# One transformer layer: the last attention group finished behind its last values, and the sequence branch worked by halves of the tokens

## The chip, the cores and the metric

One core of a Trainium2 chip runs the whole layer in one launch. The metric is device time in microseconds, lower is better. Engines: TensorE (matmul, transpose; PE in the profile), VectorE (DVE), ScalarE (ACT), GpSimd (POOL), SyncE (SP, which issues most DMAs). Each engine works through its own queue in order and waits on semaphores; nothing reorders the program but the person who wrote it.

## The reference

All data are float32: x is 2 x 1024 x 256 (two sequences of 1024 tokens).

```
c  = mixture(x, cond)                 # top 2 of 4 experts per sequence, plus a shared expert
q, k, v = split(c @ w_qkv.T)          # 16 heads of 16; q, k root-mean-square normed
y  = softmax(q k.T / 4) v
y  = y - (y . vn) vn                  # vn = v / |v|
x2 = x + y @ w_proj.T
conv = conv_b + x2[t-1] * cond[0] + x2[t] * cond[1]      # two taps, per channel
b  = softplus(conv @ Wp[:, :64] + bp);  c = tanh(conv @ Wp[:, 64:] + bp)
u  = x2 @ Ws + bs
s[t] = decay * s[t-1] + dt * b[t] * u[t]                 # decay, dt from A_log, dt_log
x3 = (c * s) @ Wo + bo
r  = sigmoid(x3 @ Wr + br);  e = argmax r                # one of 8 experts per token
out = x2 + max(r) * (gelu(x3 @ W1[e]) @ W2[e])
```

## The kernel before

The layer runs in four stages: the mixture with the projection to q, k, v (0 to about 330 us), attention (to 572), the part in question (572 to 651), and the routed experts (to the end).

*Attention.* Eight groups of work, each of four heads of one sequence. A group's output is accumulated in banks 6 and 7 of PSUM, copied to SBUF by VectorE (`take_output`), turned back by TensorE (`turn`), and finished by VectorE (`finish_group`, lines 1311 to 1327: divide by the row sums, product with v, sum, scale, subtract) into `ctx_tm`.

*Output projection and residual.* The 16 tiles of 128 tokens go in eight pairs w = 0 to 7, four to a sequence. For each pair TensorE turns the context (`turn_ctx`, L1788, to bank 0 or 1), ScalarE copies it (L906), TensorE multiplies by the projection (`project`, L1799, to bank 4 or 5), and VectorE adds x in place (`add_x`, L1349). Pairs 0 to 3 belong to the first sequence, whose context was complete long before; pairs 4 to 7 wait for the last group.

*Sequence branch.* `turn_x2(w)` (L1809) turns x2 to channels by tokens, one bank for each pair of channel half `w % 2` and 512 tokens `w // 2`. ScalarE reads each bank twice: the present tap with its bias (L913) and a plain copy (L915). VectorE adds the past tap (`past_tap`, L1037). Then TensorE makes three projections of 2 x 512 tokens: u from x2, b and c from the taps (L1864). The two sequences take the lower and upper 64 partitions, so one instruction of the gates and of the scan works on both sequences, and `n` = 0, 1 is the first and second 512 tokens of both. So both halves of the tokens need pairs of both sequences. The gates use Exp and Ln (softplus) and Tanh on ScalarE; the scan is one VectorE instruction for each half (L1394).

*Logits.* Not x3 but the scan's result times the product Wo x Wr gives the logits (L1897). That product, and the constant part from bo and br, are made by TensorE (L1833 to L1843, bank 0) with ScalarE's copies (L927, L932) and a VectorE add (L1373). Then VectorE routes (from L1402), and x3 is stored and gathered again by expert.

*Order around the change, in the version before.* VectorE's queue: copies of the last group's values, `add_x` 0 to 2, `finish_group`, `add_x` 3, past taps of sequence 0 (1,023 tokens each), `add_x` 4 to 7, past taps of sequence 1, then the gates. TensorE's queue after the last values: pairs 0 to 3 of context and projection, with the last group's turns between; x2 turns 0 to 3; pairs 4 to 7 with x2 turns 4 and 5 between; Wo; x2 turns 6 and 7; the router product; then

```
pe.wait_ge(x2T_out, TT // 2)
for k, w, src in ((1, ws_sb[:], x2T), (0, wp_sb[:, :, 0:N], convT), (2, wp_sb[:, :, N:2 * N], convT)):
    if k == 0:
        pe.wait_ge(conv_done, NB)
        pe.wait_ge(wowr_out, NB + 1)
```

and `keep_warm(9)` (L1850): nine products of constants into bank 6 which nobody reads, each of two matmul instructions in the trace; they keep TensorE busy while VectorE and ScalarE work. The biases of x3 (`bias_x3`, L1874) and the logits stand behind it.

*Transfers.* SP stores x2 when each sequence's residual is done (L601), then loads the weights of four experts (L584, L586), waits for the stores of x3 (issued by ScalarE, L960), and loads the others. GpSimd gathers x3 rows (L724) when the token numbers are known (L1456) and x3 is stored. ScalarE begins to read the experts' weights (L978) behind the stores of x3 in its queue.

Of the kernel before, what the change touches and what calls it, by code (L numbers as in the profile page):

```python
# [40 lines left out]
HG = 4  # L41
# [28 lines left out]
def layer_kernel(nc, a, out):  # L70

    with ExitStack() as ctx:
# [288 lines left out]
        seq_step = sem("seq_step")  # L361
        decay_step = sem("decay_step")
# [390 lines left out]
        def _(act):  # L753
# [163 lines left out]
            for w in range(4):  # L917
                ctx_to_sbuf(w)
            for w in range(4):
                x2_to_sbuf(w)  # L920
            for w in range(4, 7):
                ctx_to_sbuf(w)
            x2_to_sbuf(4)
            x2_to_sbuf(5)
            ctx_to_sbuf(7)
            act.wait_ge(wo_turned, 1)
            act.copy(woT[:].rearrange("p k n -> p (k n)"), bank(0)[:, 0:C]).then_inc(wo_out, 1)  # L927
            x2_to_sbuf(6)
            x2_to_sbuf(7)
            act.wait_ge(wowr_made, 1)  # L930
            for b in range(NB):
                act.copy(wowr[half[b], b, :], bank(0)[half[b], C:C + RE]).then_inc(wowr_out, 1)  # L932


            for n in range(2):
                c = slice(512 * n, 512 * n + 512)
                act.wait_ge(neg_abs, n + 1)
                act.activation(gate_e[:, c], gate_e[:, c], ACT.Exp).then_inc(soft_exp, 1)
            act.wait_ge(decay_e, 1)
            act.activation(decay[:, 2:4], decay[:, 2:4], ACT.Ln, bias=1.0).then_inc(decay_e, 1)  # L940
            for n in range(2):
                c = slice(512 * n, 512 * n + 512)
                act.wait_ge(soft_exp, n + 1)
                act.activation(gate_e[:, c], gate_e[:, c], ACT.Ln, bias=1.0).then_inc(soft_log, 1)
            for n in range(2):
                c = slice(512 * n, 512 * n + 512)
                act.wait_ge(seq_made, 5 + n)
                act.activation(gate_c[:, c], bank(4 + n), ACT.Tanh, bias=bp_c[:, 0:1]).then_inc(tanh_done, 1)
# [76 lines left out]
        def _(dve):  # L1025
# [271 lines left out]

            def take_output(g):
# [47 lines left out]
            def add_x(w):  # L1346
                dve.wait_ge(proj_made, w + 1)
                two = x_tm[:, 2 * w:2 * w + 2, :]
                dve.tensor_tensor(two, bank(4 + w % 2).rearrange("p (i c) -> p i c", i=2), two, ALU.add)\  # L1349
                    .then_inc(x2_done, 1)  # L1350


            def past_tap(b):
                dve.wait_ge(x2T_out, 4 * b + 4)
                for c in range(CK):
                    s = slice(b * L + 1, (b + 1) * L)
                    ins = stt(convT[:, c, s], x2T[:, c, b * L:(b + 1) * L - 1], cond_col[:, c, 0:1],
                              convT[:, c, s], ALU.mult, ALU.add)
                ins.then_inc(conv_done, 1)
# [5 lines left out]
            add_x(3)  # L1365
            past_tap(0)
            for w in range(4, TT // 2):
                add_x(w)
            past_tap(1)


            dve.wait_ge(wowr_out, NB)
            dve.tensor_tensor(blr_row[:], bank(0)[:, C + RE:C + 2 * RE], br_row[:], ALU.add).then_inc(wowr_out, 1)  # L1373
            link = chain(seq_step)
            for n in range(2):
                c = slice(512 * n, 512 * n + 512)
                dve.wait_ge(seq_made, n + 1)
                link(dve.tensor_scalar(seq_u[:, c], bank(2 + n), bs_col[:, 0:1], None, ALU.add))
            for n in range(2):
                c = slice(512 * n, 512 * n + 512)  # L1380
                dve.wait_ge(seq_made, n + 3)
# [3 lines left out]
            dve.wait_ge(decay_e, 2)  # L1385
            link(stt(decay[:, 4:6], decay[:, 0:2], 0.0, decay[:, 2:4], ALU.max, ALU.add))
            link(dve.tensor_tensor(decay[:, 6:7], decay[:, 4:5], decay[:, 5:6], ALU.mult))
            link(dve.tensor_scalar(decay[:, 6:7], decay[:, 6:7], -1.0, 1.0, ALU.mult, ALU.add))
            for n in range(2):
                c = slice(512 * n, 512 * n + 512)  # L1390
                dve.wait_ge(soft_log, n + 1)
                link(stt(gate_b[:, c], gate_b[:, c], 0.0, gate_e[:, c], ALU.max, ALU.add))
                link(stt(gate_b[:, c], gate_b[:, c], decay[:, 5:6], seq_u[:, c], ALU.mult, ALU.mult))
# [3 lines left out]
                dve.tensor_tensor(seq_u[:, c], gate_e[:, c], gate_c[:, c], ALU.mult).then_inc(state_out, 1)  # L1397

# [120 lines left out]
        def _(pe):  # L1519
# [264 lines left out]
            def turn_ctx(w):  # L1784
                pe.wait_ge(ctx_done, 4 if w < 4 else 8)
# [6 lines left out]
            pe.wait_ge(exp_done, UNITS * GROUPS)  # L1792
            turn_ctx(0)
# [19 lines left out]
            for w in range(4):  # L1813
                if w < 3:
                    turn_ctx(w + 1)
                project(w)
                if w == 0:
                    for h in range(2):
                        turn(GROUPS - 1, h)
            for w in range(4):  # L1820
                turn_x2(w)
            turn_ctx(4)
            for w in range(4, TT // 2):
                if w + 1 < TT // 2:
                    turn_ctx(w + 1)
                project(w)
                if w == 5:
                    turn_x2(4)
                    turn_x2(5)
            pe.wait_ge(late_in, 16 * LATE)  # L1830
            pe.wait_ge(ctxT_out, TT // 2)
            for c in range(CK):
                ins = pe.transpose(bank(0)[:, c * P:(c + 1) * P], wo_sb[:, c * P:(c + 1) * P], ident[:])  # L1833
            ins.then_inc(wo_turned, 1)
            turn_x2(6)
            turn_x2(7)
            pe.wait_ge(bo_spread, 1)
            pe.wait_ge(wo_out, 1)
            for c in range(CK):
                ins = pe.matmul(bank(0)[:, C + RE:C + 2 * RE], bo_wide[:, c, :], wr_sb[:, c, :],  # L1840
                                start=(c == 0), stop=(c == CK - 1))
# [175 lines left out]
```

## Time and profile before

| | |
|---|---|
| median of 3 runs | 831.3 us (831.15 to 832.24) |
| profiled execution | 830.84 us |
| its span | 829.1 us |
| PE / DVE / ACT / POOL busy | 95 / 57 / 63 / 30% of the span |
| mean granted clock | 0.99 of full speed |

Times in the rows are microseconds from the span's start. A row of the timeline gives start, duration, engine, line, operation, output<-inputs, shapes and count; in brackets how long the engine had stood idle and what ended it. The duration of several instructions in one row runs from the first one's start to the last one's end. Matmuls overlap, so a busy TensorE is not one at its peak. PEclk is the granted TensorE clock: 1.00 is 2.4 GHz, 0.50 is 1.2 GHz. A float32 matmul of the program is two instructions in the trace.

### The profile page before, as it was taken

The page shows a single profiled execution, that of the slowest core. Times are in us where ns is not written, and L with a number is a line of the kernel's source. Part 1 is how long each engine was busy: PE and PEld are TensorE (multiplying, and loading weights), DVE is VectorE, ACT ScalarE, POOL GpSimd, SP SyncE. Part 2 cuts the span into 40 slices and gives each one's busy share as a digit, 9 for nine tenths or more (in the row PEclk, how much of TensorE's full clock was granted, in tenths as well). Part 3 has the DMA queues.
Part 4 walks back from the last instruction along what each step waited for, and adds up shares of the span by engine and source line. Part 5 has one row for each costly group of instructions (what it writes and reads, how often), then busy time and mean ns, then how long its engine had stood idle before and what let it go on. Part 6 is the DMA issues. An engine that isn't in the chain of part 4 may idle for free.

```text
span 829.1 us, 13128 instructions
## 1 busy us (share of the span) xinstructions
PE 791.7 (95%) x4452; PEld 519.2 (63%) x4452; DVE 468.9 (57%) x865; ACT 523.0 (63%) x696; POOL 248.3 (30%) x308
## 2 busy tenths in 40 slices
PE   8999999998999999999999999999799799999994
PEld 5778888887777877233333233234646488888884
DVE  3887666468866660652321122021466489999994
ACT  4432222463232236999999999996454288888883
POOL 5343444224433410500000001000000356777762
PEclk9999999999999999999999999999999899999999
DMA  9131111100233504055462353100197921111000
GB/s 255 19 71 59 43 35 49 51 23 29 78 126 127 102 17 60 1 77 142 88 128 38 40 77 55 23 1 1 52 326 248 377 79 51 52 49 51 25 11 1
DMA packets 52682, 64.99 MB, mean 78 GB/s; under 512 B 15889, under 2 KB 43929, under 8 KB 52636
## 3 DMA queue, kind: packets, MB, share of 16 engines
q1 hardware_dynamic: 44564, 55.96, 26.9%
q0 software_dynamic: 3312, 6.31, 2.5%
q10 hardware_dynamic: 4760, 2.12, 0.9%
q8 instruction: 27, 0.44, 0.2%
q14 instruction: 19, 0.16, 0.1%
HBM read 51.52 MB, written 15.60 MB: 81 GB/s over the span
## 4 chain that ended last, share of the span: by engine, by line
PE 80%; DVE 9%; ACT 4%; issue 3%; DMA 2%; ACTq 1%; DVEq 1%; POOLq 0%
PE psum L1608 43%; PE psum L1713 15%; PE psum L1700 12%; PE psum L1950 2%; PE psum L1850 2%; DVE w_lo L1481 2%; DVE hl L1037 1%; PE psum L1799 1%; PE psum L1864 1%; DVE hh L1186 1%; PE psum L1671 1%; ACT w_hi L978 1%; DVE ssum L1226 1%; DMA time_bias<-in_L_cond_time_b 1%; DMA xs<-x_d,token_s 1%
## 5 line engine op out<-in xcount | busy, mean ns | idle before, releaser
L824 ACT ACTIVATE pexp<-psum 128x1024 f32<-128x1024 f32 x256 | 238.6, 1151 | 7.6 <-PE psum L1700 7.4
L811 ACT ACTIVATE hid<-psum,b_col 128x512 f32<-128x512 f32 x96 | 66.0, 688 | 160.8 <-PE psum L1608 105.5
L1713 PE MATMUL psum<-pexp,v_ones 128*32 128x512 f32 x1024 | 136.4, 605 | 0.7 <-ACT pexp L824 0.7
L1700 PEld LDWEIGHTS psum<-q_stack,k_stack 48*128 48x128 f32 x512 | 45.6, 183 | 127.0 <-ACT pexp L824 109.3
L1700 PE MATMUL psum<-q_stack,k_stack 48*128 48x512 f32 x512 | 111.5, 480 | 2.9 <-DVE parts L1295 2.9
L1186 DVE TENSOR_SCALAR hh<-hid,scale_col 128x341 fp32r<-128x341 f32 x192 | 71.5, 414 | 69.5 <-ACT hid L811 52.9
L1037 DVE SCALAR_TENSOR_TENSOR hl<-hid,scale_col,hh 128x341 fp32r<-128x341 f32 x192 | 95.4, 538 | 3.4
L1302 DVE COPY yT<-psum 128x512 f32<-128x512 f32 x16 | 11.1, 691 | 131.3 <-PE psum L1713 131.3
L1608 PE MATMUL psum<-hh,w2h 128*128 128x512 f32 x192 | 76.6, 399 | 4.0 <-DVE hl L1037 3.7
L1608 PE MATMUL psum<-x_hi,w1h 128*128 128x512 f32 x192 | 77.0, 401 | 0.6 <-DVE x_lo L1051 0.5
L1608 PE MATMUL psum<-hh,w2l 128*128 128x512 f32 x192 | 75.0, 391 | 0.0
L1608 PE MATMUL psum<-x_hi,w1l 128*128 128x512 f32 x192 | 75.0, 391 | 0.0
L1608 PE MATMUL psum<-hl,w2h 128*128 128x512 f32 x192 | 74.9, 390 | 0.0
L1608 PE MATMUL psum<-x_lo,w1h 128*128 128x512 f32 x192 | 74.9, 390 | 0.0
L666 POOL CAST w1h<-raw 128x256 fp32r<-128x256 f32 x48 | 20.5, 426 | 169.4 <-PE psum L1608 154.3
L1608 PE MATMUL psum<-w_hi,fhT_hi 128*128 128x256 f32 x184 | 55.3, 300 | 5.3 <-DVE fhT_lo L1488 2.7
L1476 DVE TENSOR_TENSOR w_lo<-w_all,w_hi 128x1024 fp32r<-128x1024 f32 x44 | 52.0, 1222 | 10.5 <-ACT w_hi L978 10.5
L1481 DVE TENSOR_TENSOR w_lo<-w_all,w_hi 128x1024 fp32r<-128x1024 f32 x46 | 55.9, 1217 | 0.2 <-ACT w_hi L983 0.2
L690 POOL COPY v_ones<-v_tm 128x512 f32<-128x512 f32 x8 | 4.8, 614 | 167.0 <-PE psum L1713 167.0
L1608 PE MATMUL psum<-w_lo,fhT_hi 128*128 128x256 f32 x184 | 51.5, 280 | 0.0
L1608 PE MATMUL psum<-w_hi,fhT_lo 128*128 128x256 f32 x184 | 51.4, 279 | 0.0
L983 ACT CAST w_hi<-w_all 128x1024 fp32r (+1 forms) x46 | 48.6, 1059 | 0.8 <-PE psum L1608 0.8
(281 smaller groups left out, 1457.9 us busy)
## 6 DMA issues: line engine op xcount, KB each, us to landing
w_all<-in_L_ffn_W SPq DMA_DIRECT2D x16, 1024.0 KB, 13.0
raw<-in_L_cond_ew SPq DMA_DIRECT2D x32, 256.0 KB, 3.1
parts_d<-parts SPq DMA_DIRECT2D x8, 1024.0 KB, 4.1
q_stack<-parts_d SPq DMA_DIRECT2D x48, 128.0 KB, 4.6
k_stack<-parts_d SPq DMA_DIRECT2D x48, 128.0 KB, 7.3
raw<-in_L_cond_sw SPq DMA_DIRECT2D x16, 256.0 KB, 3.6
x_d<-x_tm SPq DMA_DIRECT2D x2, 1024.0 KB, 5.0
x_d<-x_tm ACTq DMA_DIRECT2D x4, 512.0 KB, 3.6
```

What stands on the lines that cost most here:

```text
L666: pool.tensor_copy(w1h[k][:], r1)
L811: act.activation(hid[k % 4][:], bank(k % 4), ACT.Gelu_apprx_tanh, bias=b1_col[:, bass.ds(4 * q + k // 2, 1)]).then_inc(gelu_done, 1)
L824: act.activation(pexp[mt % 2][:, 2 * j:2 * j + 2, 512 * h:512 * h + 512], psum[:, 2 * r:2 * r + 2, :], ACT.Exp, scale=D ** -0.5)\
L983: act.copy(split_quarter(w_hi, 2 + q), quarter(e, 2 + q)).then_inc(w2_hi, 1)
L1037: return dve.scalar_tensor_tensor(out=out, in0=in0, scalar=scalar, in1=in1, op0=op0, op1=op1)
L1186: ins = dve.tensor_scalar(hh[k % 4][:, x0:x1], hid[k % 4][:, x0:x1], w[r], None, ALU.mult)
L1476: dve.tensor_tensor(split_quarter(lo, h), quarter(e, h), split_quarter(hi, h).bitcast(F32), ALU.subtract).then_inc(w1_split, 1)
L1481: dve.tensor_tensor(split_quarter(w_lo, 2 + q), quarter(e, 2 + q), split_quarter(w_hi, 2 + q).bitcast(F32), ALU.subtract).then_inc(w2_spli ...
L1608: ins = pe.matmul(o, w[i], x[j], start=first and n == 0, stop=last and n == 2)
L1700: ins = pe.matmul(psum[:, 2 * r + lane, :], k_stack[i][rows, j, mt * P:(mt + 1) * P], q_stack[i][rows, j, 512 * h:512 * h + 512], start=Tr ...
L1713: ins = pe.matmul(psum[VW * j:VW * j + VW, 6 + h, :], v_ones[i][:, mt, j, :], pexp[mt % 2][:, j, 512 * h:512 * h + 512], start=(mt == 0), ...
L1850: pe.matmul(bank(6), ident[:], projT[:].rearrange("p k c -> p (k c)"), start=(k == 0), stop=(k == n - 1))
```

## The change

`finish_group` takes a function that it calls at two places, so that the last group starts at once and residual adds 0 and 1 stand inside it. Wo and the router product go from behind the pairs to the first pair, in bank 3 in place of bank 0; the x2 turns then wait for the bias row. The pairs go two by two. A past tap is now one channel half of 512 tokens (eight in place of four of 1,023), each counted. The six groups of projections (three kinds, two halves) have each its own waits, and their order is b0, u0, b1, c0, u1, c1. ScalarE takes Exp, Ln and Tanh by halves, and the second half's u (`second_u`), which VectorE made. Nine dummy products become one. The logits of the first half come before the second half is known.

VectorE (behind the bias row the order is residual add 2, 3, past tap 0, 1, add 4, 5, tap 2, 3, add 6, 7, tap 4, 5, and then the gates as shown):

```
-            def finish_group(b, hg):
+            def finish_group(b, hg, between=None):
...
+                if between:
+                    between(0)
                 dve.wait_ge(y_read, 2 * g + 2)
                 dve.tensor_tensor(y_dot[:], y_tm[:], v, ALU.mult).then_inc(post_step, 1)
+                if between:
+                    between(1)
...
+            def past_tap(w):
+                c, s0 = w % 2, 512 * (w // 2)
+                first = 1 if s0 % L == 0 else 0
+                dve.wait_ge(x2T_out, w + 1)
+                stt(convT[:, c, s0 + first:s0 + 512], x2T[:, c, s0 + first - 1:s0 + 511], cond_col[:, c, 0:1],
+                    convT[:, c, s0 + first:s0 + 512], ALU.mult, ALU.add).then_inc(conv_done, 1)

             take_output(GROUPS - 1)
-            for w in range(3):
-                add_x(w)
-            finish_group(1, H // HG - 1)
...
+            finish_group(1, H // HG - 1, between=add_x)
+            dve.wait_ge(wowr_out, NB)
+            dve.tensor_tensor(blr_row[:], bank(3)[:, C + RE:C + 2 * RE], br_row[:], ALU.add).then_inc(wowr_out, 1)
...
+            gate_in(0, first, 1)
+            past_tap(6)
+            past_tap(7)
+            dve.wait_ge(seq_made, 2)
+            link(dve.tensor_scalar(seq_u[:, first], bank(2), bs_col[:, 0:1], None, ALU.add))
+            dve.wait_ge(decay_e, 2)
...
+            gate_in(1, second, 3)
+            states(0, first)
+            states(1, second)
```

ScalarE (behind the evictions, whose order is context 0, 1, Wo, context 2, 3, router product, x2 0, 1, context 4, 5, x2 2, 3, context 6, 7, x2 4 to 7):

```
+            half_exp(0, first)
             act.wait_ge(decay_e, 1)
             act.activation(decay[:, 2:4], decay[:, 2:4], ACT.Ln, bias=1.0).then_inc(decay_e, 1)
...
+            half_log(0, first)
+            half_exp(1, second)
+            output_gate(0, first, 4)
+            half_log(1, second)
+            act.wait_ge(seq_made, 5)
+            act.activation(seq_u[:, second], bank(3), ACT.Identity, bias=bs_col[:, 0:1]).then_inc(second_u, 1)
+            output_gate(1, second, 6)
```

TensorE (between the router product and the wait for the bias row stand context turns 2, 3 and projections 2, 3; behind the wait x2 turns 0, 1, context turns 4, 5, x2 turns 2, 3, projections 4, 5, context turns 6, 7, x2 turns 4, 5, projections 6, 7):

```
+            turn_ctx(0)
+            turn_ctx(1)
+            output_matrix()
+            for h in range(2):
+                turn(GROUPS - 1, h)
+            project(0)
+            project(1)
+            output_times_router()
...
+            pe.wait_ge(wowr_out, NB + 1)
...
+            def sequence(k, n):
+                w, src = ((wp_sb[:, :, 0:N], convT), (ws_sb[:], x2T), (wp_sb[:, :, N:2 * N], convT))[k]
+                pe.wait_ge(x2T_out, 6 if n == 0 else TT // 2)
+                if k != 1:
+                    pe.wait_ge(conv_done, 6 if n == 0 else TT // 2)
...
+            turn_x2(6)
+            turn_x2(7)
+            for k, n in ((0, 0), (1, 0), (0, 1), (2, 0), (1, 1), (2, 1)):
+                sequence(k, n)
-            keep_warm(9)
...
+            bias_x3(0)
+            make_logits(0)
+            pe.wait_ge(second_u, 1)
+            bias_x3(1)
+            keep_warm(1)
+            pe.wait_ge(tanh_done, 2)
+            bias_x3(2)
+            make_logits(1)
```

## Rows read from the trace of the kernel before

**Rows 1.** Chain that ended last, 560 to 660: start, duration, what.

```profile
572.37 0.60 PE psum L1788 x4
...
585.29 0.69 DVE ctx_tm L1327
...
615.84 7.92 PE psum L1850 x18
623.76 1.58 PE psum L1874 x6
625.34 1.89 PE psum L1897 x16
...
643.49 0.19 DVE token_s L1456
...
644.64 6.43 DMA xs<-x_d,token_s
```

**Rows 2.** Timeline of VectorE, 570 to 628: start, duration, instruction, [idle before].

```profile
572.43 0.69 DVE L1302 COPY yT<-psum 128x512 f32<-128x512 f32 x1 [1.07 <-PE psum L1713]
...
581.53 0.25 DVE L1311 RECIPROCAL y_r<-psum 128x16 f32<-128x16 f32 x1
...
582.89 0.69 DVE L1318 TENSOR_TENSOR y_dot<-y_tm,v_tm 128x512 f32<-128x512 f32 x1
...
601.33 0.69 DVE L1349 TENSOR_TENSOR x_tm<-psum,x_tm 128x512 f32<-128x512 f32 x1 [1.69 <-PE psum L1799]
605.21 2.48 DVE L1037 SCALAR_TENSOR_TENSOR convT<-x2T,cond_col,convT 128x1023 f32<-128x1023 f32 x2 [3.19 <-ACT x2T L915]
...
610.80 0.75 DVE L1382 TENSOR_SCALAR gate_b<-psum,bp_b 128x512 f32<-128x512 f32 x1 [0.97 <-PE psum L1864]
...
618.24 1.22 DVE L1394 TENSOR_TENSOR_SCAN gate_e<-decay,gate_b 128x512 f32<-128x512 f32 x1
...
622.93 0.69 DVE L1397 TENSOR_TENSOR seq_u<-gate_e,gate_c 128x512 f32<-128x512 f32 x1
627.27 0.29 DVE L1402 TENSOR_TENSOR route<-psum,blr_row 128x128 f32<-128x128 f32 x1 [3.64 <-PE psum L1897]
```

**Rows 3.** Timeline of TensorE, 575 to 616.

```profile
575.51 1.04 PE L1671 MATMUL psum<-ident,yT 128*128 128x128 f32 x8
...
576.83 1.89 PE L1799 MATMUL psum<-projT,ctxT 128*128 128x256 f32 x8
...
586.73 1.85 PE L1809 MATMUL psum<-ident,x_tm 128*128 128x128 f32 x8 [3.25 <-DVE x_tm L1349]
...
605.32 3.65 PE L1864 MATMUL psum<-x2T,ws_sb 128*64 128x512 f32 x16 [1.36 <-ACT x2T L915]
608.77 7.07 PE L1864 MATMUL psum<-convT,wp_sb 128*64 128x512 f32 x32
```

**Rows 4.** Timeline of ScalarE, 593 to 616.

```profile
593.18 0.58 ACT L906 COPY ctxT<-psum 128x512 f32<-128x512 f32 x1 [2.03 <-PE psum L1788]
...
602.77 0.78 ACT L913 ACTIVATE convT<-psum,convb_col,cond_col 128x512 f32<-128x512 f32 x1 [0.85 <-PE psum L1809]
...
603.91 0.79 ACT L913 ACTIVATE convT<-psum,convb_col,cond_col 128x512 f32<-128x512 f32 x1
...
613.96 0.63 ACT L938 ACTIVATE gate_e<-gate_e 128x512 f32<-128x512 f32 x1 [1.01 <-DVE gate_e L1037]
614.61 1.28 ACT L940 ACT_TABLE_LOAD   x1
```

**Rows 5.** Windows: stretch, length, busy time, clock, DMA share, GB/s.

```profile
620.00:632.00 12.00, 12.00 (x57) 7.87 (x57) 5.95 (x16) 3.48 (x6) 0.00 (x0) 0.86 0.81 280
...
588.00:590.00 2.00, 2.00 (x11) 1.88 (x9) 0.00 (x0) 2.00 (x4) 0.00 (x0) 0.50 1.04 347
```

**Rows 6.** DMA issues in the timelines of ScalarE's and SP's queues.

```profile
635.37 0.93 ACTq L960 DMA_DIRECT2D x_d<-x_tm  x2
...
639.85 0.37 SPq L584 DMA_DIRECT2D w_all<-in_L_ffn_W  x1
```

More of the change, by code:

```diff
@@ L915, in x2_to_sbuf @@
                 act.copy(x2T[:, c, s], x2_bank(w)).then_inc(x2T_out, 1)
[L917 to L925, printed above, removed]
+            ctx_to_sbuf(0)
+            ctx_to_sbuf(1)
             act.wait_ge(wo_turned, 1)
-            act.copy(woT[:].rearrange("p k n -> p (k n)"), bank(0)[:, 0:C]).then_inc(wo_out, 1)
@@ L928, in _ @@
-            x2_to_sbuf(6)
-            x2_to_sbuf(7)
+            act.copy(woT[:].rearrange("p k n -> p (k n)"), bank(3)[:, 0:C]).then_inc(wo_out, 1)
+            ctx_to_sbuf(2)
+            ctx_to_sbuf(3)
             act.wait_ge(wowr_made, 1)
             for b in range(NB):
-                act.copy(wowr[half[b], b, :], bank(0)[half[b], C:C + RE]).then_inc(wowr_out, 1)
-            for n in range(2):
-                c = slice(512 * n, 512 * n + 512)
+                act.copy(wowr[half[b], b, :], bank(3)[half[b], C:C + RE]).then_inc(wowr_out, 1)
@@ L937, in _, with half_exp, half_log @@
+            x2_to_sbuf(0)
+            x2_to_sbuf(1)
+            ctx_to_sbuf(4)
+            ctx_to_sbuf(5)
+            x2_to_sbuf(2)
+            x2_to_sbuf(3)
+            ctx_to_sbuf(6)
+            ctx_to_sbuf(7)
+            for w in range(4, 8):
+                x2_to_sbuf(w)
+            first, second = slice(0, 512), slice(512, 1024)
+            def half_exp(n, c):
                 act.wait_ge(neg_abs, n + 1)
                 act.activation(gate_e[:, c], gate_e[:, c], ACT.Exp).then_inc(soft_exp, 1)
+            def half_log(n, c):
+                act.wait_ge(soft_exp, n + 1)
+                act.activation(gate_e[:, c], gate_e[:, c], ACT.Ln, bias=1.0).then_inc(soft_log, 1)
@@ L939, in _, with output_gate @@
+            def output_gate(n, c, made):
+                act.wait_ge(seq_made, made)
+                act.activation(gate_c[:, c], bank(4 + n), ACT.Tanh, bias=bp_c[:, 0:1]).then_inc(tanh_done, 1)
+            half_exp(0, first)
             act.wait_ge(decay_e, 1)
             act.activation(decay[:, 2:4], decay[:, 2:4], ACT.Ln, bias=1.0).then_inc(decay_e, 1)
[L941 to L944, printed above, removed]
@@ L1368, in _ @@
+            for w in range(4, 6):
                 add_x(w)
-            past_tap(1)
-            dve.wait_ge(wowr_out, NB)
-            dve.tensor_tensor(blr_row[:], bank(0)[:, C + RE:C + 2 * RE], br_row[:], ALU.add).then_inc(wowr_out, 1)
-            link = chain(seq_step)
[L1375 to L1378, printed above, removed]
@@ L1379, in _, with gate_in @@
-            for n in range(2):
-                c = slice(512 * n, 512 * n + 512)
-                dve.wait_ge(seq_made, n + 3)
+            for w in range(2, 4):
+                past_tap(w)
+            for w in range(6, TT // 2):
+                add_x(w)
+            for w in range(4, 6):
+                past_tap(w)
+            link = chain(seq_step)
+            first, second = slice(0, 512), slice(512, 1024)
+            def gate_in(n, c, made):
+                dve.wait_ge(seq_made, made)
@@ L1389, in _, with states @@
-            for n in range(2):
-                c = slice(512 * n, 512 * n + 512)
+            def states(n, c):
                 dve.wait_ge(soft_log, n + 1)
                 link(stt(gate_b[:, c], gate_b[:, c], 0.0, gate_e[:, c], ALU.max, ALU.add))
+                if n:
+                    dve.wait_ge(second_u, 1)
                 link(stt(gate_b[:, c], gate_b[:, c], decay[:, 5:6], seq_u[:, c], ALU.mult, ALU.mult))
@@ L1811, in turn_x2 @@
                 ins.then_inc(x2_turned, 1)
[L1813 to L1821, printed above, removed]
-            turn_ctx(4)
[L1823 to L1841, printed above, removed]
@@ new lines, in output_times_router @@
+            def output_times_router():
+                pe.wait_ge(bo_spread, 1)
+                pe.wait_ge(wo_out, 1)
+                for c in range(CK):
+                    ins = pe.matmul(bank(3)[:, C + RE:C + 2 * RE], bo_wide[:, c, :], wr_sb[:, c, :],
+                                    start=(c == 0), stop=(c == CK - 1))
+                for c in range(CK):
+                    ins = pe.matmul(bank(3)[:, C:C + RE], woT[:, c, :], wr_sb[:, c, :],
+                                    start=(c == 0), stop=(c == CK - 1))
+                ins.then_inc(wowr_made, 1)
```

95 lines of the change are left out of this document (48 added, 47 removed).

## The prediction

> **What bounds the kernel now.** Three views, in this order. First the chain that ended last, between the end of attention and the first expert tile [rows 1]. The reader is to see a serial stretch in which no engine is full: TensorE's first context turn at 572.37, the last group's context written by VectorE at 585.29, 18 dummy matmuls from 615.84, biases, logits at 625.34, token numbers at 643.49, and a gather to 651.07. Then the timelines by engine [rows 2 to 4], for durations and for who waits: VectorE starts to finish the context at 581.53, though the turns of its values were issued from 575.51 on and over at 576.55, because three residual adds stand ahead of it in its queue; the scans' last product ends at 623.62 (622.93 + 0.69); routing begins at 627.27. Last the windows and the DMA issues [rows 5, 6].
>
> The profiled execution took 830.84 us (span 829.1 and 1.7 around it), 0.46 below the median of 831.3. The sum is made against 830.84, from the point at which the last values end in both kernels (572.37) to the routing add, 627.27 now. What is computed behind that add is not touched.
>
> **The change, walked with durations of the rows.** The same walk made with the old order ends at 626.4, 0.8 short; 0.6 of it is the stretch with the clock at 0.50 [rows 5], so I trust such a walk to about 0.3. Its steps: four turns occupy TensorE 0.44 (0.11 each), one projection of eight matmuls 1.74, and 0.25 more pass until its result is seen [rows 3]; a hand-over between engines costs 0.03.
>
> *Context.* On TensorE two context turns and the two turns of the output matrix end at 573.4; the value turns wait for VectorE's second copy (572.43 + 0.69 [rows 2]) and end at 574.4. Projections 0 and 1, now behind them, are seen at 576.3 and 578.0. VectorE divides as soon as the turns are there, 574.0 to 575.35 (1.36 from 581.53 to 582.89 now [rows 2]). Residual add 0, now inside, waits for projection 0 and ends at 577.0. The rest took 3.09 from the product at 582.89 to 585.98 (585.29 + 0.69 [rows 1]); it starts at 576.9, and add 1 inside it, waiting for projection 1, adds 1.1: 581.0. Gain 5.0, net of 1.0 and 0.4 of waiting at the two adds.
>
> *Output matrix and router product.* Moved ahead. TensorE issues 2 turns and 8 narrow matmuls (1.1, by 0.11 each as a turn [rows 3]), ScalarE three short copies (each below the 0.58 of a full one [rows 4]) between context copies; they hold the third context copy until 579.3, under VectorE's tail. The new wait for the router's bias row, ahead of the first turn of x2, holds all of TensorE's queue: the projections, taps and groups behind it. The row is there at 581.1 and TensorE arrives at 583.4, behind projections 2 and 3, so it costs nothing; a row later than 583.4 would cost its whole lateness.
>
> *To the last residual add.* ScalarE paces: the two evictions of one x2 turn cost 1.14 (602.77 to 603.91 [rows 4]), a context copy 0.49 to 0.58. First pairs 584.0 to 586.4, context 4 to 586.9, so projections 4 and 5 run from 586.9 to 590.7; next pairs and contexts 6 and 7 to 592.1, projections 6 and 7 to 596.0, last add seen at 596.75, where it is 602.02 (601.33 + 0.69 [rows 2]). Gain 5.3. TensorE's 3.25 of idling ahead of 586.73 and the half clock behind it [rows 3, 5] go; the walk has no gap over 1.3.
>
> *Taps and projections by halves.* Two taps of 1,023 elements take 2.48 [rows 2]. One of 512 lies between half of one (0.62) and the biased read of 512 (0.75); I take the 0.69 of a product of 512. Taps 4 and 5 end at 597.97 and the first of six groups of eight matmuls starts at 598.0; a group takes 1.77 (7.07 for four [rows 3]). Now the first group starts at 605.32: gain 7.3. Two groups run to 601.5; the third waits for tap 7. ScalarE's last evictions end at 599.8, VectorE reads the first gate in between (0.75 + 0.69), so tap 7 ends at 602.72: 1.2 of TensorE standing still. The last four groups run from 602.75 to 609.8, where the old ones end at 615.84: gain 6.0.
>
> *Gates.* ScalarE changes function tables four times before the logits where it did twice (Ln; Exp with Tanh; Ln; Tanh). A change is a row of 1.28 that starts 0.02 behind the Exp before it [rows 4]; I take 1.29. Exp 0 runs 601.5 to 602.2; table; Ln 0 done 604.2; table to 605.5; Exp 1, when VectorE is ready, 606.3 to 606.9; Tanh 0 to 607.6; table to 608.8; Ln 1 to 609.4; the second half's biased copy, which was VectorE's, to 610.1; table; Tanh 1 to 612.0. Tanh and copy lie between a copy and a scaled, biased one (0.58 and 0.78 [rows 4]); 0.68, the middle. VectorE has the second gate by 606.25, the first half's states from there to 609.7 (0.69 + 0.75 + 1.22 + 0.69 and hand-overs, by [rows 2], the sum of two inputs as the product), the second's from 609.64 to 613.1. ScalarE's results come before VectorE wants them, but by only 0.25 (Ln 1), 0.26 (copy) and 0.4 (Tanh 1). So the two additional loads cost nothing; without that cover 1.3 each.
>
> The Trainium skill, "ScalarE: Activation LUTs", section "What ACT_TABLE_LOAD costs", counts a drain of 1.38 with each load, 2.66 in all, and its "Rules for kernel authors" say to do all of one set before switching: a rule against this order. No drain is seen in the row above, 0.02 from the Exp's end to the load [rows 4]. By the page's figure the walk ends 4.1 later, by the row it doesn't move.
>
> *Logits.* The 18 dummies (7.92 [rows 1]) become 2 (0.88); the biases (1.58 for three) and the logits (1.89) go by halves among them, 609.8 to 613.25, just as the last states come at 613.1, and the last eight logits end at 614.3. Routing add at 614.33, with the walk's shortfall 614.5, against 627.27: gain 12.7.
>
> *Behind it.* Two things can give a little back. The experts' weight loads stand behind the last residual add, so they start only 5.3 earlier than now, and they fill the DMA engines for some 27 us (0.81 of the 12 us from 620, so until about 629.6 [rows 5]), in the changed kernel until 624.3. The stores of x3, the second pair of which is issued at 635.37 and done at 639.85, when SP goes on [rows 6], come 12.7 earlier and share the engines with the loads' last 5 us. They end between 627.2 (not held up) and 633.3 (loads first, then twice 4.5), against token numbers at 630.9 (643.67 - 12.7): cost 0 to 2.4, most likely near 0, since sharing only lengthens the first pair. And the clock is low for 3.4 us behind the old logits (0.86 of 12 us [rows 5]); that stretch will sit elsewhere. I take 0.3 for both: net 12.4, 818.4 against 830.84, 818.7 against the median.
>
> **Rivals.**
> *A low clock in the new stretch.* It fell behind 3.25 us of idling, and behind the light biases and logits that followed full dummies [rows 1, 3, 5]. The dummies go from 18 to 2, and the light work spans 4.5 us. At half clock the last bias and logits cost 1.6 more, all from the second bias on 3.0, the whole tail 4.5, the two groups before the gap 2.9. Against: the old low stretch falls on the x3 matmuls; moved, it leaves them. 820.5 to 823.2.
> *ScalarE becomes the bound.* If a table change cost twice its row (2.57), the walk ends 3.8 later: 822.5. It decides as soon as a change costs 0.15 more. Against: the rows. The skill's page named above describes this case.
> *x3 stores behind the weight loads*, which hold up gather and first tile: 2.4, 820.8.
> *Only the first part arrives.* If the experts' weights paced what follows, only the loads' 5.3 would remain: 825.5. Against: the first four experts' loads end at 629.6, before ScalarE first reads weights, which stands behind the store issue of 635.37.
> *Slower.* One mechanism: the clock falls in the gaps between 596 and 603 and, with the dummies gone, does not come back. All six groups (1.77 more each), biases and logits run at half; logits end at 628.9, 1.7 later than now: 832.5, and later still if the dummies behind the ranking are slow too. It decides from five slow groups together with the tail. Against: now the groups start at 605.32 behind 1.36 of idling [rows 3] and keep the full clock.
>
> **How the numbers follow.** Forecast 62% (own range 816.5 to 820.5), low clock 18%, ScalarE 6%, stores 6%, only the first part 4%, slower 4%. The range 815.5 to 823.3: at the lower end the forecast without any low stretch (half of 3.4, 1.7 less) without its 0.3, and less the walk's whole shortfall of 0.8; at the upper the clock and table cases. Some 10% is left out. A difference of 0.2%, 1.7 us, is about what can be told; of the cases only the lower end of the slower one lies so near to no change. Faster 0.94, same 0.02, slower 0.04.
>
> **What would show it.** Counted from the first context turn: context written 8.6 after it, last residual add 24.4, first group 25.6, third group 30.4, last states 40.7, routing add 42.0. Two more table loads stand between the first Exp and the last Tanh, and VectorE idles for ScalarE by no more than 0.3 behind its second gate. The prediction is wrong if VectorE's states wait for ScalarE by over 1 us, if the granted clock is under 0.9 between 597 and 614, or if the gather starts more than 1.5 behind the token numbers.

## The result, and the profile after

The changed kernel takes 820.56 us (median of four, 818.73 to 821.23) against 831.34; ratio 0.9868, interval 0.9848 to 0.9887. The forecast was 818.7. The profiled execution took 820.85, span 819.1.

All stage times below are counted from the first context turn after the last values, which is 572.30 in the trace of before and 571.89 here (the front of the kernel varies by itself: this turn lies between 571.2 and 574.8 in the traces). These are the two rows, first of before, then of after:

```profile
572.30 1.09 PE L1788 MATMUL psum<-ident,ctx_tm 128*128 128x128 f32 x8
571.89 1.09 PE L1818 MATMUL psum<-ident,ctx_tm 128*128 128x128 f32 x8
```

| counted from the first context turn | before | forecast | after |
|---|---|---|---|
| last group's context written | 13.7 | 8.6 | 8.6 |
| last residual add | 29.7 | 24.4 | 24.5 |
| first group of projections | 33.0 | 25.6 | 25.9 |
| last states | 51.3 | 40.7 | 41.2 |
| routing add | 55.0 | 42.0 | 43.6 |
| token numbers | 71.4 | 58.7 | 60.9 |
| first gather landed | 78.8 | 66.4 | 69.4 |

(The prediction gives no distance for the last two: 58.7 is the old distance less the walk's 12.7, 66.4 the old one less the net 12.4.) Counted from the first turn to the end of the span the gain is 9.6: of the 10.0 between the profiled executions, 0.4 is the front. VectorE first. These rows of its timeline answer to [rows 2]: the context's last product, the last residual add, three of the second half's state operations, the routing add.

```profile
579.84 0.69 DVE L1351 TENSOR_TENSOR ctx_tm<-y_tm,y_dot 128x512 f32<-128x512 f32 x1
...
595.72 0.69 DVE L1314 TENSOR_TENSOR x_tm<-psum,x_tm 128x512 f32<-128x512 f32 x1 [1.03 <-PE psum L1827]
...
609.53 0.68 DVE L1050 SCALAR_TENSOR_TENSOR gate_b<-gate_b,gate_e 128x512 f32<-128x512 f32 x1
610.25 0.75 DVE L1050 SCALAR_TENSOR_TENSOR gate_b<-gate_b,decay,seq_u 128x512 f32<-128x512 f32 x1
...
612.36 0.69 DVE L1412 TENSOR_TENSOR seq_u<-gate_e,gate_c 128x512 f32<-128x512 f32 x1
615.51 0.29 DVE L1430 TENSOR_TENSOR route<-psum,blr_row 128x128 f32<-128x128 f32 x1 [2.46 <-PE psum L1944]
```

The second half's states run 609.53 to 613.05 without a wait. ScalarE's timeline (that of before is [rows 4]) shows why there is none: the second Ln and the biased copy end at 609.42 and 610.00, just ahead of 609.53 and 610.25, and the last Tanh at 612.00, ahead of 612.36, with a table load of 1.28 in front of each group, 0.01 from the load's end to the Ln.

```profile
607.50 1.28 ACT L946 ACT_TABLE_LOAD   x1
608.79 0.63 ACT L946 ACTIVATE gate_e<-gate_e 128x512 f32<-128x512 f32 x1
609.33 0.67 ACT L960 ACTIVATE seq_u<-psum,bs_col 128x512 f32<-128x512 f32 x1
610.02 1.28 ACT L950 ACT_TABLE_LOAD   x1
611.31 0.69 ACT L950 ACTIVATE gate_c<-psum,bp_c 128x512 f32<-128x512 f32 x1
```

The chain of waits, answering to [rows 1]: two groups of projections, 1.23 of standing still for the last taps, four groups, then biases (L1922), logits (L1944) and one dummy product (L1891), the x3 products (L1930), token numbers and gather.

```profile
597.83 3.65 PE psum L1908 x16
601.49 1.23 issue
602.71 7.09 PE psum L1908 x32
609.80 0.66 PE psum L1922 x2
610.46 0.99 PE psum L1944 x8
611.45 0.66 PE psum L1922 x2
612.11 1.06 PE psum L1891 x2
613.16 0.66 PE psum L1922 x2
613.82 1.65 PE psum L1944 x8
615.47 3.72 PE psum L1930 x16
...
632.61 0.19 DVE token_s L1484
...
633.77 7.49 DMA xs<-x_d,token_s
```

The reader is to see two things. The second logits (613.82) start 0.77 behind the last states (613.05): TensorE's own queue is late. And eight logits that took 0.99 at 610.46 take 1.65 at 613.82. The windows, answering to [rows 5], say why: the granted clock is at 0.99 up to 614 and at 0.50 from there.

```profile
612.00:614.00 2.00, 2.00 (x7) 0.84 (x7) 1.01 (x2) 1.28 (x1) 0.00 (x0) 0.99 1.07 397
614.00:620.00 6.00, 6.00 (x28) 4.80 (x27) 2.00 (x8) 2.15 (x5) 0.00 (x0) 0.50 1.06 380
620.00:626.00 6.00, 6.00 (x27) 3.18 (x27) 5.01 (x21) 2.85 (x6) 1.07 (x4) 0.93 1.08 368
```

The low stretch lasts 6.8 us, to 620.8, and covers the sixteen x3 products (3.72) and the ranking; its old counterpart was 3.4 long [rows 5]. SP goes on to the later weight loads at 630.69, 1.9 ahead of the token numbers at 632.61; the second stores of x3 were issued at 624.52, so they took 6.2 where they took 4.5 [rows 6]. They did not hold up the gather, but they put off the later loads by 1.7.

```profile
630.69 0.37 SPq L585 DMA_DIRECT2D w_all<-in_L_ffn_W  x1
```

### The profile page after: what moved, and what is told of

Same layout as the page of the kernel before. It is cut to its first block, busy times and chain, and to the rows that moved or that the text cites. A ratio compares the mean times of both kernels' runs of the same rounds, so it can differ in the third digit from the quotient of the medians.

```text
span 819.1 us, 13104 instructions
## 1 busy us (share of the span) xinstructions
PE 784.3 (96%) x4436; PEld 515.1 (63%) x4436; DVE 467.9 (57%) x868; ACT 526.1 (64%) x699; POOL 248.4 (30%) x308
## 4 chain that ended last, share of the span: by engine, by line
PE 85%; DVE 7%; issue 2%; ACT 2%; DMA 2%; SPq 0%; ACTq 0%; DVEq 0%; POOLq 0%
PE psum L1636 46%; PE psum L1741 15%; PE psum L1728 12%; PE psum L2006 2%; PE psum L1827 2%; DVE hl L1050 1%; PE psum L1908 1%; DVE hh L1199 1%; PE psum L1699 1%; PE psum L1891 1%; DMA xs<-x_d,token_s 1%; DMA x_tm<-in_x 1%; DVE ssum L1239 1%; PE psum L1930 1%; DVE w_lo L1509 1%
## 5 line engine op out<-in xcount | busy, mean ns | idle before, releaser
L1199 DVE TENSOR_SCALAR hh<-hid,scale_col 128x341 fp32r<-128x341 f32 x192 | 69.8, 405 | 69.6 <-ACT hid L812 52.7
L1636 PE MATMUL psum<-w_hi,fhT_lo 128*128 128x256 f32 x184 | 51.3, 279 | 0.0
```

What stands on the lines that cost most here:

```text
L1199: ins = dve.tensor_scalar(hh[k % 4][:, x0:x1], hid[k % 4][:, x0:x1], w[r], None, ALU.mult)
L1636: ins = pe.matmul(o, w[i], x[j], start=first and n == 0, stop=last and n == 2)
```

## The experiments

Times are medians; "the kernel before" in the same rounds had 830.8 to 832.2. A kernel's runs spread over 1.1 to 5.3 us, so a difference of medians under about 1 us is not taken for one; there the profile is read, counted from the first context turn. The changed kernel was not run again in these rounds, so beside its median its ratio to the kernel before (0.9868, 0.9848 to 0.9887) is to be compared.

**The context early, in either kernel.** First the changed kernel with adds 0 and 1 ahead of the finishing:

```
-            finish_group(1, H // HG - 1, between=add_x)
+            for w in range(2):
+                add_x(w)
+            finish_group(1, H // HG - 1)
```

> The changed kernel with residual adds 0 and 1 put back ahead of the finishing of the last group. Theory A (the order of the pairs and ScalarE's evictions pace this stretch, the early context has slack): the context is written about 2 us later, 582.7 in place of 580.5, which is still before TensorE comes to the fifth context turn at 583.9; the time stays at 820.6 within 0.4. Rival B (finishing directly behind the last values is a good part of the gain): everything behind moves with the context, 2.1 us later, 822.7.

Measured: 820.67 (818.67 to 821.64), ratio 0.987 (0.9848 to 0.9892). VectorE's timeline, from a first turn at 571.19:

```profile
581.24 0.69 DVE L1351 TENSOR_TENSOR ctx_tm<-y_tm,y_dot 128x512 f32<-128x512 f32 x1
...
614.92 0.29 DVE L1432 TENSOR_TENSOR route<-psum,blr_row 128x128 f32<-128x128 f32 x1 [2.56 <-PE psum L1946]
```

The context is written at 10.7 in place of 8.6, the routing add comes at 43.7 in place of 43.6. So theory A holds: nobody waits for the early context. Then the kernel before with nothing but the early context:

```
-            for w in range(3):
-                add_x(w)
             finish_group(1, H // HG - 1)
-            add_x(3)
+            for w in range(4):
+                add_x(w)
```

> The kernel before with the last group finished directly behind its last values on VectorE, ahead of the residual adds 0 to 2, and nothing else. Theory A (the context has slack where TensorE's order is not changed with it): the context is written 5.3 earlier, 580 in place of 585.3, the last residual add not, and the routing add stays 55.0 behind the first context turn, within 0.7; 831. Rival B (the early context is what the change lives on): 3 to 5 earlier, 826 to 828.

Measured: 833.42 (831.68 to 836.42), ratio 1.0016 (1.0003 to 1.0029): no gain, rather a small loss. The context is there at 8.4, but the third projection needs the bank that residual add 0 frees, and that add now stands behind the finishing. TensorE's timeline, from a first turn at 573.39:

```profile
582.53 3.69 PE L1798 MATMUL psum<-projT,ctxT 128*128 128x256 f32 x16 [2.28 <-DVE x_tm L1349]
...
588.00 1.04 PE L1787 MATMUL psum<-ident,ctx_tm 128*128 128x128 f32 x8
591.96 3.31 PE L1798 MATMUL psum<-projT,ctxT 128*128 128x256 f32 x8 [2.92 <-ACT ctxT L906]
...
608.25 4.16 PE L1863 MATMUL psum<-x2T,ws_sb 128*64 128x512 f32 x12 [1.36 <-ACT x2T L915]
```

TensorE waits 2.28 there and 2.92 for ScalarE behind it, and the next projection takes 3.31 in place of 2.0, at the half clock. The last residual add comes at 31.6, where it was 29.7. The first two groups (the last row has twelve of their sixteen matmuls) take 5.35, at a low clock (0.71 in the mean of 608.2 to 614), where they took 3.65 behind the same gap of 1.36 [rows 3]. Rival B falls, and theory A's "within 0.7" of the routing add as well: it comes at 58.5.

**The front alone.** The changed kernel up to the x2 turns, then the sequence branch of before (whole tokens, nine dummy products, biases, both logits).

```
-            for k, n in ((0, 0), (1, 0), (0, 1), (2, 0), (1, 1), (2, 1)):
-                sequence(k, n)
+            for k, w, src in ((1, ws_sb[:], x2T), (0, wp_sb[:, :, 0:N], convT), (2, wp_sb[:, :, N:2 * N], convT)):
...
+            keep_warm(9)
```

> The changed kernel up to the last x2 turn, and from there the sequence branch of before: u, b, c for whole tokens, Exp, Exp, Ln, Ln, Tanh, Tanh, nine dummy products, biases, then both halves' logits. Theory A (the gain of the walk is 5.3 up to the last residual add and the rest from the halves and the dummies): routing add 5.3 to 5.7 earlier than in the kernel before, 825.5 to 826. Rival B (the halves only use time that the front gives, and the front alone brings nearly all): under 822. Rival C (the dummies set the end, so what comes earlier ahead of them is lost in another wait): over 828.

Measured: 825.38 (824.72 to 827.15), ratio 0.9936 (0.9916 to 0.9955): 5.4 of the gain, as theory A has it for the time. The last residual add is at 24.5 (595.47 + 0.69, from 571.64), 5.2 earlier than in the kernel before. The routing add is not where theory A has it: at 51.5 (623.12), 3.5 earlier and not 5.3 to 5.7. TensorE's timeline:

```profile
599.46 5.35 PE L1889 MATMUL psum<-x2T,ws_sb 128*64 128x512 f32 x16 [2.15 <-ACT x2T L916]
```

Behind 2.15 of idling the first two groups took 5.35 in place of 3.65, with the granted clock at 0.50 from 602 to 604. Behind the logits it stayed at 1.00 (616 to 630), where the kernel before was low for 3.4; there the end gets back what the routing add lacks. So the 5.4 hold two places of the low clock. They are the work of the whole front: the order of the pairs on three engines, Wo and the router product moved ahead, and taps by halves; no run separates these.

**The early start of the first half.** All six groups wait for all evictions, those of b and c for all taps as well, and VectorE reads the first gate behind the last tap:

```
-                pe.wait_ge(x2T_out, 6 if n == 0 else TT // 2)
+                pe.wait_ge(x2T_out, TT // 2)
...
-                    pe.wait_ge(conv_done, 6 if n == 0 else TT // 2)
+                    pe.wait_ge(conv_done, TT // 2)
...
-            gate_in(0, first, 1)
             past_tap(6)
             past_tap(7)
+            gate_in(0, first, 1)
```

> The changed kernel, but the groups of the first half wait for all evictions and all taps, and VectorE reads the first gate behind the last tap. Theory A (TensorE stands still 1.2 us between the halves anyway, and the gates' chain is bound by VectorE and ScalarE, so the early start of the first half is worth little): first group about 600.3 in place of 597.8, the six groups without a gap, last states 1.6 later, the last logits 1.0 later, since TensorE's queue has 0.7 of its own: 821.6. Rival B (what starts 2.5 later ends 2.5 later): 823.1.

Measured: 821.22 (820.47 to 824.35), ratio 0.9877 (0.9857 to 0.9897). By the medians 0.7, near theory A's 1.0, but within the spread. The profiled execution is the slowest of the five (824.35) and shows another cost:

```profile
600.56 3.68 PE L1908 MATMUL psum<-convT,wp_sb 128*64 128x512 f32 x8 [2.90 <-ACT x2T L916]
604.00 3.09 PE L1908 MATMUL psum<-x2T,ws_sb 128*64 128x512 f32 x8
606.91 3.61 PE L1908 MATMUL psum<-convT,wp_sb 128*64 128x512 f32 x16
```

Behind 2.90 of idling the first two groups run at half clock (3.68 and 3.09 in place of 1.94 and 1.92). So an early first half also fills a gap in which the clock may fall; how often it does without it, one trace does not tell.

**The dummies.** The kernel before with one dummy product in place of nine:

```
-            keep_warm(9)
+            keep_warm(1)
```

> The kernel before with one dummy product in place of nine, nothing else. Theory A (TensorE's queue, filled with dummies to 623.76 and biases to 625.3, set the logits 1.7 later than the states at 623.62 allowed, so part of the gain of the change is the fewer dummies alone): logits of the first half ahead of the last states, routing add up to 2.6 earlier at full clock; after some 5 us with little work the clock will be low, which takes back 1 to 2: 829 to 830. Rival B (the dummies keep the clock, and without them logits, x3 and ranking at half clock cost more than the queue gives): 831.5 to 834.

Measured: 830.16 (827.51 to 832.16), ratio 0.9983 (0.9967 to 0.9999). Theory A, at the lower end of its gain (its time was 829 to 830): the routing add comes at 53.4 in place of 55.0, and the end gains 1.4 (1 - 0.9983 of 831.65). Then the changed kernel without its one dummy product:

```
-            keep_warm(1)
```

> The changed kernel without its one dummy product. Theory A (TensorE's queue is 0.7 late for the last logits, and the dummy takes 1.06 of it): last logits start 0.65 earlier, 820.0. Rival B (the dummy holds the clock): the low clock begins before the last logits and takes 1 us or more, 821 to 822.

Measured: 818.84 (816.89 to 821.32), ratio 0.9847 (0.9823 to 0.9872). TensorE's timeline of the tail, from a first turn at 573.54:

```profile
612.05 1.06 PE L1944 MATMUL psum<-wowr,seq_u 128*128 128x16 f32 x8
613.04 1.39 PE L1922 MATMUL psum<-bo_split,ones_r 2*128 2x512 f32 x4
614.76 1.06 PE L1944 MATMUL psum<-wowr,seq_u 128*128 128x16 f32 x8 [0.33 <-DVE seq_u L1412]
```

The second logits now wait 0.33 for the states, not the other way round; both logits take 1.06, and the routing add (615.87) is at 42.3, 1.3 earlier. Here the clock fell only behind the logits, at 615.8. The queue part, 0.7, is theory A; the rest is where the low stretch fell. The token numbers come 2.1 earlier, but the gather behind them takes 7.81, and by medians alone the intervals overlap with the changed kernel's.

**Useful work in the dummy's place.** The first x3 product needs only the first half's states:

```
             make_logits(0)
+            make_x3(0)
             pe.wait_ge(second_u, 1)
             bias_x3(1)
-            keep_warm(1)
-            pe.wait_ge(tanh_done, 2)
-            bias_x3(2)
             make_logits(1)
-            make_x3(0)
             make_x3(1)
+            pe.wait_ge(tanh_done, 2)
+            bias_x3(2)
```

> The changed kernel with the first x3 product in the place of the dummy product, and the third pair of biases and the second x3 product behind the last logits. Theory A (TensorE's queue, not the states, sets the last logits: they start at 613.75 where the states are there at 613.05, and the x3 products stand in the way of the ranking's matmuls at half clock): routing add 0.7 to 1.4 earlier, the ranking's matmuls 2.0 to 2.5 earlier, about 818.3. Rival B (the low clock follows the light work wherever it stands and takes the same time again): no difference over 0.7.

Measured: 821.25 (818.85 to 823.27), ratio 0.9867 (0.9845 to 0.9888). Both theories are half right. TensorE's timeline, from a first turn at 573.62:

```profile
614.84 1.06 PE L1944 MATMUL psum<-wowr,seq_u 128*128 128x16 f32 x8
615.84 2.06 PE L1930 MATMUL psum<-wo_sb,seq_u 64*128 64x256 f32 x8
617.82 1.22 PE L1922 MATMUL psum<-bo_split,ones_r 2*128 2x512 f32 x2
618.97 0.80 PE L1961 MATMUL psum<-rt,tri 128*128 128x128 f32 x2
...
625.28 9.24 PE L1891 MATMUL psum<-projT,ident 128*128 128x512 f32 x16
633.96 2.27 PE L1974 MATMUL psum<-tile_hot,lane_hot 128*128 128x72 f32 x16
```

The second logits start at 41.2 (changed kernel 41.9) and at full clock, the ranking's matmuls at 45.4 (47.2): 1.9 earlier, near theory A's 2.0 to 2.5. But in this execution, the slowest of the five (823.27), the low clock lasts 13.7 us, from 615.9, and the sixteen dummy matmuls behind the ranking take 9.24 in place of 7.13; the token matmuls wait behind them. With five in place of eight products there:

```
-            keep_warm(8)
+            keep_warm(5)
```

> The kernel with the first x3 product in the place of the dummy product and biases and second x3 product behind the last logits, and with five dummy products in place of eight behind the ranking. Theory A (in the earlier run the logits did come 1.3 earlier and the ranking 1.9, but sixteen dummy matmuls, part of them at half clock, then held TensorE's queue 2 us beyond VectorE's lanes): token numbers 2 earlier than in the changed kernel counted from the last values, 818.6. Rival B (with fewer dummies the clock falls again at once and the token matmuls and the first tile pay): 820.5 or more.

Measured: 819.24 (819.03 to 822.23), ratio 0.9865 (0.9838 to 0.9891). The row of the token numbers (631.38, from a first turn at 572.72) starts at 58.7, 2.1 earlier than the changed kernel's at 60.7. Of that the median shows 1.3, inside the spread, and the ratio next to nothing: the gather took 7.87. Not all of the difference to the run above is the dummies' work. The low clock lasted 6.8 us here and was over at 621.7, ahead of 623.17, where the first of the dummy products starts; up to them the two kernels are the same.

**One more change of table.** A square root of one element between Tanh 0 and Ln 1:

```
             output_gate(0, first, 4)
+            act.activation(act_warm[:], ones[0:1, 0:1], ACT.Sqrt)
             half_log(1, second)
```

> The changed kernel with one more change of ScalarE's function tables: a square root of one element between the first Tanh and the second Ln, whose result nobody reads. Theory A (a change costs its row of 1.28 and no drain; ScalarE is only 0.1 to 0.4 ahead of VectorE there): Ln and copy 1.5 later, last states 1.4 later, last logits 0.7 later because TensorE's queue was 0.7 late by itself: 44.3 us from the first context turn to the routing add, where the changed kernel has 43.6; 821.3. Rival B (a change drains the engine, 2.66): last states 2.7 later, routing add 45.7 behind the first turn, 822.7.

Measured: 820.70 (819.86 to 821.75), ratio 0.9865 (0.9844 to 0.9885). ScalarE's timeline, and VectorE's behind it:

```profile
606.25 0.67 ACT L950 ACTIVATE gate_c<-psum,bp_c 128x512 f32<-128x512 f32 x1
606.93 1.28 ACT L958 ACT_TABLE_LOAD   x1
608.23 0.20 ACT L958 ACTIVATE act_warm<-ones 1x1 f32<-1x1 f32 x1
608.43 1.28 ACT L946 ACT_TABLE_LOAD   x1
609.73 0.63 ACT L946 ACTIVATE gate_e<-gate_e 128x512 f32<-128x512 f32 x1
```

```profile
610.39 0.69 DVE L1051 SCALAR_TENSOR_TENSOR gate_b<-gate_b,gate_e 128x512 f32<-128x512 f32 x1 [1.34 <-ACT gate_e L946]
...
613.23 0.69 DVE L1413 TENSOR_TENSOR seq_u<-gate_e,gate_c 128x512 f32<-128x512 f32 x1
```

Each load follows the instruction before it within 0.02 and is itself followed within 0.02. VectorE waits 1.34 for Ln, and its last states end at 42.6 behind the first turn, 1.44 later than in the changed kernel: load and root (1.28 + 0.20) less ScalarE's lead of 0.1 there, no drain. The routing add is at 44.7, 1.1 later, between the two expectations, because the last biases ran at half clock there. The end shows none of it: the low clock was over ahead of the ranking, whose first product took 0.49, and the gather took 7.03. The Trainium skill, "ScalarE: Activation LUTs", section "What ACT_TABLE_LOAD costs", has 2.66 for a change with its drain; this trace does not agree, the change costs 1.3.

**The gather and the weight loads.** The loads of experts 4 to 6 start behind the first gathers:

```
                 if e == 4:
                     sp.wait_ge(x3_stored, 16 * 2 * NB)
+                    sp.wait_ge(tokens_known, 1)
+                    for i in range(2):
+                        sp.wait_ge(xs_in[i], 16)
+                    sp.wait_ge(x2s_in[0], 16)
```

> The changed kernel, but SP begins the weight loads of experts 4 to 6 only when the first two gathers of x3 rows and the first of x2 rows have landed. Theory A (the first gather takes 7.49 us, 1.06 more than before, because it shares the DMA engines with these loads; the later gathers take 3.4): the gather takes 3.4 to 4.0, the first expert tile starts 3.5 to 4 earlier, the weights still come 10 us and more before they are read: 816.8 to 817.3. Rival B (the gather's time is GpSimd's own, for writing its descriptors): 7 us again, 820.6. Rival C (the later loads hold up tiles 4 to 7): first tile earlier, end not.

Measured: 817.94 (816.81 to 819.24), ratio 0.984 (0.9816 to 0.9865). The chain of waits:

```profile
633.80 3.48 DMA xs<-x_d,token_s
...
637.32 0.45 PE psum L1988 x2
...
656.93 6.69 DMA xs<-x_d,token_s
```

The gather takes 3.48 in place of 7.49, with the DMA share at 0.15 to 0.29 from 634 to 640, where it was 1.05 from 634 to 641; so theory A and not B. TensorE stands idle for a shorter time, and the low clock that followed the gather in the changed kernel (0.66 in the mean of 640 to 650) does not come: 1.00. Yet the end gains 2.6 by medians, not 4, and the intervals of the two ratios still touch: the loads now meet a later gather (DMA share 1.03 to 1.09 from 654 to 664, where it was 0.25 from 655 to 665), which takes 6.69 and is waited for. So rival C holds in part.

**Together.** Early x3, five dummies and loads behind the gather, that is the edits of three runs above in one kernel:

```
+            make_x3(0)
             pe.wait_ge(second_u, 1)
             bias_x3(1)
-            keep_warm(1)
...
-            keep_warm(8)
+            keep_warm(5)
...
+                    sp.wait_ge(tokens_known, 1)
...
```

> The kernel with the early x3 product, five dummies behind the ranking, and the weight loads of experts 4 to 6 behind the first gathers. If the two gains are in stretches that follow each other, token numbers 2.0 earlier and the gather 4 shorter: 815.8. If the shorter gather only brings the wait for the third tile's gather forward (it took 6.69 in the run with the later loads), 817.5 to 818.

Measured: 816.63 (816.24 to 818.31), ratio 0.9814 (0.9796 to 0.9832). Then no dummy, and loads behind the gather:

```
-            keep_warm(1)
...
+                    sp.wait_ge(tokens_known, 1)
...
```

> The changed kernel without its one dummy product and with the weight loads of experts 4 to 6 behind the first gathers. If both gains (1.7 and 2.6 between medians) add up: 816.2. If the first came only from where the low clock happened to fall: 817.5 to 818.

Measured: 816.86 (815.18 to 817.76), ratio 0.9813 (0.9794 to 0.9832). The gains add up for the most part; both beat the changed kernel by some 4 us with intervals that do not touch its own. Of the first, the median is 0.8 short of the 815.8 expected, and the later gather is still waited for (6.48); by the ratio (0.9814 of 831.34 is 815.9) nothing is short, so whether that wait costs anything here is open.

## Why the prediction was right, and by what it was off

The forecast was a gain of 12.4; the medians give 10.8, the two profiled executions 10.0. A slip of the prediction's sum made it look larger: 12.4 off the median of 831.3 is 818.9, not 818.7. The measured 820.56 lies 0.06 above the forecast's own range (816.5 to 820.5), where the range of the low-clock rival begins (820.5 to 823.2), and what the forecast missed is in part that rival. None of the three signs against the prediction came: VectorE did not wait for ScalarE's results of the second half, the clock was at 1.00 from 597 to 614, and the gather started 1.0 behind the token numbers.

*Context, last add, first group.* Right to 0.3: 8.6, 24.5 and 25.9 against 8.6, 24.4 and 25.6. The share that the prediction gives to the early context ("Gain 5.0") is right as a time of that step, but it is not what the end gains by: the changed kernel without it is as fast, the kernel before with it is not faster. The front's 5.4 come from what else was changed there, above all in the order.

*The bias row's wait* cost nothing, as forecast. The add behind the context was done at 580.60 and the first x2 turn issued at 583.04.

*Taps and groups.* The gap of 1.2 between the halves was 1.23. A tap of 512 took 0.75 alone and 0.70 each in a pair; 0.69 was taken. That the groups kept the full clock was less sure than the prediction says: behind the same gap of 1.36 that it argues from, the clock fell in the kernel with the early context alone.

*Gates.* In the second half ScalarE was ahead of VectorE by 0.1 to 0.4, as forecast (ahead of the second gate VectorE waited 0.30 for the logarithm of the decay, which cost nothing, since TensorE's group came later still); the rival by which ScalarE becomes the bound does not occur, and the run with one more change gives the price of a change beyond that cover.

*Logits.* The first term that was mis-sized. The walk had the second logits start 0.15 behind the last states and take 1.05; they started 0.77 behind and took 1.65. The biases took 0.66 a pair and the dummy product 1.06, where the walk divided whole rows (0.53 and 0.88), and the clock fell at 614.0. This is the first rival's mildest case ("the last bias and logits cost 1.6 more"). Together 1.2 of the 1.7 by which the routing add is late; the rest was there already at the last states.

*Behind it.* The second, and the larger: "I take 0.3 for both". From the routing add to the token numbers 0.9 more, since the low clock was twice as long as the old one and lay on the x3 products and the ranking; without the dummy, where it was over before the ranking, this distance was the old one again (16.5, before 16.4). In the gather 1.06 more. That the later loads are the gather's excess is shown, since without them it takes 3.48. How long it is goes with when they begin. Over the profiled executions of all these kernels: 3.6 to 4.4 ahead of the token numbers (six kernels) the gather took 6.2 to 6.6, 1.9 to 2.2 ahead (three, the changed kernel among them) 7.0 to 7.5, and together with them (two) 7.8 and 7.9. The loads begin when x3 is stored, and here the prediction had the rival right and its effect wrong: 630.69 lies inside the forecast's 627.2 to 633.3 and ahead of the token numbers, but the stores shared the engines with the first loads (DMA share 1.09 from 624 to 628), landed 1.7 late, and so moved the later loads nearer to the gather. In the same way 0.3 and 0.4 of the 2.1 that the token numbers gained without the dummy, and with the early x3 and five dummies, went into a longer gather.

*Fewer dummies* were a part of the gain that the prediction did not price by itself. Alone they are worth 1.6 at the routing add of the old kernel and 1.4 at its end (interval 0.1 to 2.7). Of the whole 10.8, 5.4 are the front by its own run; what is left by subtraction, 5.4, is the sequence branch with its fewer dummies and early first logits. The early start of the projections is a smaller part of it (0.7 by medians, not separable from the spread); the early first logits were not tried alone.

## What to carry to other kernels

Walk the chain with durations from the rows and count from a fixed point: the stages up to the last states came within half a microsecond. Then price what follows the edited stretch, too: a stage that comes earlier meets transfers that do not, and a low clock can fall on it that used to lie elsewhere. Before crediting an early result with a gain, ask who is waiting for it. And look at dummy matmuls on the critical queue: taking the last one out brought the routing add 1.3 forward, and so did work that was due anyway in its place; what of that reached the end lies near the spread (by medians from 0.7 lost to 1.7 gained).

## What the runs showed of the hardware

The clock fell without idling just before: in the changed kernel TensorE's rows follow each other from 602.71 on, from 609.80 biases of two rows, logits of sixteen columns and one dummy product, and it went from 0.99 to 0.50 at 614.0, for 6.8 us. That the light work is the reason is likely and was not tested by itself. Nor does the order of work fix the length: with the first x3 product in the dummy's place the low stretch lasted 13.7 us in one trace and 6.8 in another, whose kernel is the same up to its end. One trace tells where the clock fell, not where it will fall.

One gather of 128 rows took 3.48 us by itself and 6.2 to 7.9 beside the weight loads, though it is issued by another engine's queue. The Trainium skill, "Trainium Kernel Development and Optimization", section "Key Constraints", says that what the queues of SyncE, ScalarE and GpSimd issue runs on the same sixteen DMA engines; the trace agrees, and this is its price here.
